# Windowed attention between two feed-forward layers on one core: scores in four 64x64 tiles, masked quarters left out, and values one head later

## The reference

```
x = x + 0.5 * ffn(layernorm(x))      # ternary weights, 256 -> 1024 -> 256, gelu, rms norms
x = x + attn(layernorm(x))           # 16 heads of 64
x = x + 0.5 * ffn(layernorm(x))
```

```
q_idx = jnp.arange(bl)[:, None]; k_idx = jnp.arange(3 * bl)[None, :]   # bl = 128
rel = k_idx - bl - q_idx
valid = (jnp.abs(rel) <= LOCAL_RADIUS) & (k_pos >= 0) & (k_pos < L)    # LOCAL_RADIUS = 127
logits = einsum("bnqhd,bnkhd->bnhqk", qb, k_cat) + bias                # 512 keys a block
probs = exp(logits - m) / (sum(exp(logits - m)) + exp(-m))
```

## Time and profile before

| | |
|---|---|
| time, 3 runs | 2178.49, 2184.44, 2189.72 us, median 2184.44 |
| the profiled execution's own time | 2183.18 us |
| its span, first to last instruction | 2181.5 us |
| granted TensorE clock, mean | 0.991 |
| first and last transpose of probabilities issued | 327.3 and 1917.4 us |
| PE, DVE, ACT, POOL busy, share of the span | 94%, 86%, 88%, 64% |

### The profile page before, as it was taken

One profiled execution on the slowest core, in us unless ns is written; L12 is line 12 of the kernel. 1 busy time (PEld: TensorE's weight loads), 2 busy tenths in 40 slices (PEclk: granted clock), 3 DMA queues, 4 the chain that ended last, 5 costly groups with the idle time before them and its releaser, 6 DMA issues. The chain is left out here.

```text
span 2181.5 us, 77479 instructions
## 1 busy us (share of the span) xinstructions
PE 2049.6 (94%) x30286; PEld 1567.5 (72%) x30286; DVE 1879.6 (86%) x4646; ACT 1930.1 (88%) x4210; POOL 1406.1 (64%) x1455
## 2 busy tenths in 40 slices
PE   5999979999999999999999999999999999979999
PEld 3666657777777777777777778777777777746666
DVE  7999968889998898898979899998889889867776
ACT  5899958999999899999989999998999999969997
POOL 2444536777787687777767777786777777722221
PEclk9999989999999999999999999999999999989999
DMA  7888837999999899999989999999999999958998
GB/s 210 154 156 153 158 61 124 172 166 176 171 173 171 132 174 170 172 178 168 171 143 162 172 174 169 178 179 152 149 171 172 169 177 175 163 87 177 179 179 182
DMA packets 1341581, 355.54 MB, mean 163 GB/s; under 512 B 1321760, under 2 KB 1340192, under 8 KB 1341216
## 3 DMA queue, kind: packets, MB, share of 16 engines
q1 hardware_dynamic: 1341216, 350.59, 100.4%
HBM read 14.68 MB, written 8.39 MB: 11 GB/s over the span
## 5 line engine op out<-in xcount | busy, mean ns | idle before, releaser
L1013 POOL TENSOR_TENSOR probs_split<-probs,probs_split 128x512 f16<-128x512 f32 (+1 forms) x1026 | 1159.3, 1130 | 385.3 <-ACT probs_split L1302 281.3
L1286 ACT ACTIVATE probs<-probs,minus_max 128x512 f32<-128x512 f32 (+1 forms) x1027 | 717.0, 698 | 27.1 <-DVE minus_max L1354 26.9
L1354 DVE CUSTOM_DVE_ANT_0 probs<-score_ps,mask,neg_qk_scale 128x512 f32<-128x512 f32 (+1 forms) x1028 | 723.5, 716 | 9.6 <-PE score_ps L1125 8.3
L1147 PEld LDWEIGHTS y_ps<-v_parts,probsT 128*128 128x128 f16 x11904 | 457.7, 98 | 149.4 <-DMA probsT<-probs_split 71.1
L1147 PE MATMUL y_ps<-v_parts,probsT 128*128 128x64 f16 x11904 | 514.8, 193 | 51.4 <-DMA probsT<-probs_split 49.8
L1302 ACT ACTIVATE probs_split<-probs 128x512 f16<-128x512 f32 (+1 forms) x770 | 470.2, 611 | 8.5 <-DMA probsT<-probs_split 0.3
L1122 PE MATMUL score_ps<-k_parts,q_parts 64*128 64x384 f16 (+3 forms) x2604 | 371.1, 286 | 4.7 <-DVE k_parts L1346 2.7
L1125 PE MATMUL score_ps<-k_parts,q_parts 64*128 64x384 f16 (+3 forms) x2604 | 371.1, 286 | 0.0
L1122 PEld LDWEIGHTS score_ps<-k_parts,q_parts 64*128 64x128 f16 x2604 | 200.5, 94 | 108.0 <-issue 13.2
L1054 PE MATMUL item_ps<-b_xT,wk_split 128*128 128x128 f16 x3168 | 221.7, 220 | 1.9 <-DVE v_parts L1346 1.5
L1054 PE MATMUL item_ps<-wo_split,yT_parts 128*128 128x256 f16 x1560 | 213.9, 274 | 6.1 <-DVE v_parts L1346 4.6
(11 more groups left out here) (172 smaller groups left out, 3452.1 us busy)
## 6 DMA issues: line engine op xcount, KB each, us to landing
probsT<-probs_split SPq DMA_TRANSPOSE x1025, 3.9
out_x<-x_resident SPq DMA_DIRECT2D x64, 128.0 KB, 2.0
x_resident<-in_L_attn_x SPq DMA_DIRECT2D x56, 128.0 KB, 2.7
h_a<-in_L_ffn_w_up SPq DMA_DIRECT2D x1, 1024.0 KB, 5.8
scratch_a<-in_L_ffn_w_down SPq DMA_DIRECT2D x1, 1024.0 KB, 8.0
x_resident<-in_L_attn_x SPq DMA_DIRECT2D x2, 512.0 KB, 9.4
raw_q_a<-in_L_attn_Wq SPq DMA_DIRECT2D x1, 1024.0 KB, 11.5
raw_k_a<-in_L_attn_Wk SPq DMA_DIRECT2D x1, 1024.0 KB, 11.8
```

What stands on the lines that cost most here:

```text
L1013: nc.gpsimd.tensor_tensor(parts_of[ring(at, v)][:, LO, low_columns(place_of(at, v))], probs[v % NBUF][:, cols], parts_of[ring(at, v)][:, H ...
L1147: last = nc.tensor.matmul(out, pt[ring(at, v)][:, low * a + t, :], vr[:, slot, b, h * DH:(h + 1) * DH], start=(n == 0), stop=(n == len(pas ...
L1286: nc.scalar.activation(probs[v % NBUF][:, cols], probs[v % NBUF][:, cols], ACT.Exp, bias=bias[:, j % 2, h:h + 1], scale=-1.0, accum_out=su ...
L1354: nc.vector.tensor_tensor_reduce(out=probs[v % NBUF][:, cols], in0=score_ps[v % NBUF][:, cols], in1=mask_of(at, v), scale=w.neg_qk_scale[: ...
```

## The change

Four edits, all in `attention_phase`. (1) `scores` splits each head's queries in two sides of 64, so each matmul uses a 64x64 tile of the array, and each side leaves out the 64 keys that it can't see. (2) The ring of keys is laid out so that the tokens of one head pair adjoin (`[P, 2, NPAIR, (RING + 1) * P]`), and runs of keys may begin or end within a block. (3) The four score banks are cleared once, ahead of the first scores, as the left-out quarters are still read by the mask instruction. (4) PV_LAG goes from 3 to 4: values, the division by the denominators and the transpose of x come one slot later.

```
-    PIECES = [[(V1, 0)], [(V1, 1)], [(Q0, 0)], [(Q0, 1)], [(XTR, 0), (Q1, 0)], [(Q1, 1)], [(OUTP, 0)], [(OUTP, 1), (YT1, 0)],
+    PIECES = [[(V1, 0)], [(V1, 1)], [(Q0, 0)], [(Q0, 1)], [(Q1, 0)], [(XTR, 0), (Q1, 1)], [(OUTP, 0)], [(OUTP, 1), (YT1, 0)],
...
-    XTR_SLOT = 4
+    XTR_SLOT = 5
...
-    SCORE_AHEAD, EXP_AHEAD, SPLIT_AHEAD, TURN_AHEAD, PV_LAG = 4, 3, 2, 1, 3
+    SCORE_AHEAD, EXP_AHEAD, SPLIT_AHEAD, TURN_AHEAD, PV_LAG = 4, 3, 2, 1, 4
...
-        kr = sb("k_parts", [P, RING + 1, 2, HD], F16)
+        kr = sb("k_parts", [P, 2, NPAIR, (RING + 1) * P], F16)
...
+        def key_runs(at, v, side):
+
+            order, runs = order_of(at, v), []
+            for t, slot in tiles_of(at, v):
+                first = DH if order[t] == LEFT and side == 1 else 0
+                end = DH if order[t] == RIGHT and side == 0 else P
+                to, source, n = t * P + first, slot * P + first, end - first
+                if runs and runs[-1][0] + runs[-1][2] == to and runs[-1][1] + runs[-1][2] == source:
+                    runs[-1][2] += n
+                else:
+                    runs.append([to, source, n])
+            return runs
...
-                cols = slice(pair * P, (pair + 1) * P)
-                todo, started = tiles_of(at, v), False
-                while todo:
-
-                    (t, slot), n = todo[0], 1
-                    while n < len(todo) and todo[n][1] == slot + n:
-                        n += 1
-                    todo = todo[n:]
-                    for q_part, k_part in ((HI, HI), (HI, LO), (LO, HI)):
-                        ends = not todo and q_part == LO
-                        even = nc.tensor.matmul(score_ps[v % NBUF][:, t * P:(t + n) * P],
-                                                qs[0:DH, j % 2, q_part, cols], kr[0:DH, slot:slot + n, k_part, cols],
-                                                start=not started, stop=ends, skip_group_check=True)
-                        odd = nc.tensor.matmul(score_ps[v % NBUF + 1][:, t * P:(t + n) * P],
-                                               qs[DH:P, j % 2, q_part, cols], kr[DH:P, slot:slot + n, k_part, cols],
-                                               start=not started, stop=ends, skip_group_check=True)
-                        started = True
+                runs = [key_runs(at, v, side) for side in range(2)]
+                last = {}
+                for q_part, k_part in ((HI, HI), (HI, LO), (LO, HI)):
+                    for run in range(max(map(len, runs))):
+                        for side in range(2):
+                            if run >= len(runs[side]):
+                                continue
+                            queries = slice(pair * P + side * DH, pair * P + (side + 1) * DH)
+                            to, source, n = runs[side][run]
+                            ends = q_part == LO and run == len(runs[side]) - 1
+                            for odd in range(2):
+                                rows = slice(odd * DH, (odd + 1) * DH)
+                                last[odd] = nc.tensor.matmul(
+                                    score_ps[v % NBUF + odd][side * DH:(side + 1) * DH, to:to + n],
+                                    qs[rows, j % 2, q_part, queries], kr[rows, k_part, pair, source:source + n],
+                                    start=(run == 0 and q_part == k_part), stop=ends, skip_group_check=True)
+                even, odd = last[0], last[1]
...
+                    pe.wait_ge(scores_cleared, NBUF)
...
+            values(end, -4)
             values(end, -3)
...
-                return kr[:, slot, part, 512 * c:512 * c + 512]
+                return kr[:, part, 4 * c:4 * c + 4, slot * P:(slot + 1) * P]
...
+            for n in range(NBUF):
+                nc.vector.memset(score_ps[n][:], 0.0).then_inc(scores_cleared, 1)
...
-                    if h in (2, 10):
-                        invert_denominators(at, u - 3)
                     if h in (3, 11):
-                        normalise_y(at, u - 4, at.before(j) if h == 3 else at.item(j, YT1) + 1)
+                        invert_denominators(at, u - 4)
+                    if h in (4, 12):
+                        normalise_y(at, u - 5, at.before(j) if h == 4 else at.item(j, YT1) + 1)
```

More of the change, by code:

```diff
@@ L822, in attention_phase @@
         dve_step, cleared, half_set = sem("b_dve_step"), sem("b_cleared"), sem("half_set")
-        y_cleared = sem("y_cleared")
+        y_cleared, scores_cleared = sem("y_cleared"), sem("scores_cleared")
         block = ctx.enter_context(nc.Block())
@@ L1206, in body @@
                         block_item(at, b, j, side, (0, 1))
+                    if h == XTR_SLOT:
+                        block_item(at, b, j, XTR, (0,))
                     for kind, piece in PIECES[h]:
@@ L1209, in body @@
                             block_item(at, b, j, kind, (piece,))
-                    if h == XTR_SLOT:
-                        block_item(at, b, j, XTR, (0,))
                     if side in (SK0, SV0, SV1):
@@ L1246, in result @@
                 return bank[:, 0:KD * P].rearrange("p (k n) -> p k n", k=KD)
-            return bank[:].rearrange("p (c n) -> p c n", c=4) if kind in (YT0, YT1) else bank[:]
+            return bank[:].rearrange("p (c n) -> p c n", c=4) if kind in (YT0, YT1, *KEYS) else bank[:]
         def ring_slot(j, kind):
```

## The result

The changed kernel takes 2216.26 us in the median of 4 runs (2214.3 to 2226.56) against 2182.41 us of the kernel before (4 runs). The ratio is 1.0168, with a 95% interval of 1.0133 to 1.0203: slower by 1.7%, where 1.2% (2210 us) was forecast. The quotient of the two medians is 1.0155; the ratios in this text are those on record with their intervals, and differ from the quotients of the medians by up to 0.4%. The profiled execution took 2216.14 us, its span is 2214.4 us. Of three later kernels one execution each ran at a lower granted clock (0.66, 0.86 and 0.66 in the mean instead of 0.99) and is left out of every median and ratio here.

A forecast was written before the change was run, and what follows sets the result against it. SP's issuing of transposes was taken to bound the attention, 1.38 us each plus a stop per 16 KB of TensorE's program. 2183.2 + 32.3 - 8 + 0.8 + 0.4 = 2208.7, so 2210 us; 8-in-10 range 2140 to 2290.

The forecast's parts named there:

- SP is the limit: In the attention, SP issues 1025 transposes back to back, 1.38 us each plus fetch stops; TensorE has 62 us to spare.
- The merged row: SP's 1025 transpose issues as one timeline row: 1592.27 us before, forecast to take about 1616 us.
- The row that spoke against it: Waits table putting 521.8 us of SP down to POOL; disbelieved, since 712 issues already take 983 us of those 1100.
- The price of the fetches: Attention: 5976 more matmuls and as many loads make 47 more program fetches, 0.77 MB at 41.9 us per MB: +32.3 us.
- Shorter score matmuls are worth nothing: Attention scores: a pair takes 0.6 us, freeing PE by 20 us, none on SP's path, so priced at 0.
- rival C: Score matmuls: weight loads of the four tiles go one by one, TensorE becomes the bound, about 2280 to 2510 us; 17%.
- The lag gives 8 us back: PV_LAG 4 in the attention removes almost all of PE's 49.8 us of DMA waits: -8 us, ends 0 and -20.
- keep their distance to each other: Attention: the moved transpose of x (XTR), reciprocals and division keep their mutual distance, so cost 0.
- Clearing the banks, +0.8 us: Four clears on DVE ahead of the first low part take 1.9 us, with 1.20 us idle before it: +0.8 us.
- PE's wait for the DMA under 15 us: Before the values in the attention, PE's DMA wait should fall from 49.8 to under 15 us, the stretch no shorter.

The follow-up runs named there:

- the tiles alone: The changed kernel with PV_LAG 3 again (64x64 tiles, new ring and cleared banks only): 2209.66 us, 1.0139 of the kernel before.
- one head a DMA: Kernels issuing one transpose DMA per head; three follow-ups with one DMA for two heads measured 1.0222, 1.0290 and 1.0113 against the kernel before.
- the lag alone: The kernel before with only PV_LAG 4 and the division, transpose of x and reciprocals one slot later: 2192.63 us, 1.0059 of the kernel before.

## Why the prediction was right

**SP is the limit: right.** The merged row grew by 34.8 us and the time by 33.0 between the two profiled executions, though PE's busy time in the stretch fell by 17.5 us. Of the 34.8 us, 31.0 are longer issues and 3.8 gaps. The median issue stayed at 1.287 us. The row itself came out 11 us over the 1616 that were forecast; the tiles alone have 1616.04. Whether SP's own issuing or what the DMA engines take sets the 1.29 us was not tested. The row that spoke against it, 521.8 us of SP's waits put down to POOL, was rightly set aside: a kernel that takes 95 us of busy time off TensorE gained 29 us, and its SP row shrank almost wholly through shorter issues.

**The price of the fetches: right in size, +32.3 us forecast, and in part by luck.** 47 packets came, as counted. Summing what issues within 4.5 us of a q8 packet take over the usual 1.28 us gives 0.71 us a packet before, 0.71 after, and 0.66 to 0.74 in the other kernels with one head a DMA. 47 x 0.71 = 33 us. The tiles alone measured +1.39%, 30 us. The price of 41.9 us per MB had two errors in it that nearly cancel. It laid all of the 177.8 us on fetches, though some 28 us are gaps of SP beyond 0.09 us. And it spread them over the bytes of both queues, though those of q14 cost next to nothing. It comes to 0.69 us a packet of q8, beside the 0.71.

**Shorter score matmuls are worth nothing: right.** A burst of two pairs takes 1.28 instead of 1.42 us, 0.07 us a pair. That is 36 us over 512 pairs, more than the 20 us taken, which started from 0.64 us a pair where 0.71 is measured, and took 0.60 for the new one where 0.64 is. None of it shortened the stretch. The tiles run side by side; rival C did not happen. The Trainium skill ("TensorEngine Tiling (Array Packing)", Restrictions) has column tiling without Fast Weight Load, and the trace agrees as far as it can: loads of half the columns take 107 ns, not less than the 94 of the full width, and not the 53 ns that the prediction had for them. By the same page's Key Properties different tiles load and compute in parallel. The trace agrees, with 48 loads of 107 ns and 48 matmuls in 1.28 us.

**The lag gives 8 us back: wrong in sign.** The step that failed is the sentence that the moves of XTR, the reciprocals and the division "keep their distance to each other. 0." I compared slots (3 to 4 before, 4 to 5 after) and not places within a slot. The change also moved the transpose of x ahead of its slot's twelve projection matmuls, which take 0.68 us of PE. The division is the thing that it waits for, so PE stood still once a block, 1.1 us. That makes the +0.6% of the lag alone. In the whole change it hides almost wholly behind SP: changed against tiles only is 1.0168 against 1.0139, intervals overlapping. So of the 34 us between the medians (37 by the ratio) some 30 are the fetches; whether the rest is more than zero the runs don't decide. The total missed by about this term: 34 us between the medians, where 26 over the profiled execution were summed up.

**Clearing the banks, +0.8 us: doesn't show.** The first transpose of probabilities is issued at 326.98 us, no later than the 327.33 before.

**PE's wait for the DMA under 15 us: wrong.** It fell only to 27.9 us in the change, and to 0.2 in the lag alone. With SP further behind, landings come late enough to be met even one slot later; the tiles alone raise that wait to 86.0 us.

## What to carry to other kernels

Read the queue that issues the DMAs like an engine: when its issues and the usual gap between them add up to nearly the whole stretch (1468.7 + 1024 x 0.09 = 1561 of 1592 us here), and work lies ready before each issue, it is the limit, however busy TensorE looks. The merged timeline row alone doesn't tell, as it hides gaps. In a program written out in full, an edit that doubles the number of instructions of one kind lengthens what must be fetched, and here, with the issuing of DMAs at the limit, each fetch of 16 KB cost some 0.7 us; count instructions as well as columns. When a step moves by a slot, compare its place within the slot with what it waits for, not only the slot numbers.

## What was not expected of the hardware

- A packet of 16 KB of TensorE's program is followed by a stop of all transposes of 1.1 to 1.2 us in every kernel here with one head a DMA (204 packets and 234 us of stops before, 249 and 287 after), of which SP loses 0.7. What in the DMA system stops is not shown by these traces.
- A longer program for GpSimd, fetched by 8 KB on q14, cost little or nothing: 24 packets more, +0.12% (-0.05% to +0.28%).
- A transpose of 6 or of 8 tiles costs SP 1.24 to 1.29 us. One of 16 tiles took 1.315 us at the least but 2.07 in the median, so the price of an issue is neither fixed nor in proportion to its size.
